# Two layers of cross attention and mixture of experts on one core: a group's whole chain placed ahead of the other group's expert blocks

## The reference, cut to what matters

```
x = x + xattn0(layernorm(x), ctx)      # 16 heads of 8, rope, masked softmax
x = x + ffn0(layernorm(x))             # 32 routed experts of 64 and 8 empty ones, top 6
x = x + xattn1(layernorm(x), ctx)      # 1 head of 128, padding mask; V is the context itself
x = x + ffn1(layernorm(x))             # below

def ffn1(x):
    xn  = rms_norm(x, scale)
    ids = argmin(dist2(xn, centroids))            # one of 8 experts for each token
    for e in range(8):
        a, g = split(xn @ up_w[e])                # 128 -> 2 x 256
        y = (a * silu(g)) @ down_w[e]             # 256 -> 128
        out = where(ids == e, y, out)
    return out + x
```

## Time and profile before

| | us |
|---|---|
| runs | 311.01, 307.35, 305.27 (median 307.35) |
| the profiled execution | 305.88 |
| its span | 304.1 |
| TensorE busy | 258.1 (85%) |
| VectorE busy | 182.0 (60%) |
| ScalarE busy | 123.9 (41%) |
| GpSimd busy | 86.4 (28%) |
| mean TensorE clock | 0.907 of full speed |

### The profile page before, as it was taken

How to read it: one execution, slowest core, us unless ns; L and a number is a source line. 1 busy time by engine, 2 the same in 40 slices (tenths; PEclk the granted TensorE clock), 3 DMA queues, 4 the chain that set the end, 5 groups by cost and what they waited for, 6 DMA issues and landing times.

```text
span 304.1 us, 4365 instructions
## 1 busy us (share of the span) xinstructions
PE 258.1 (85%) x1420; PEld 159.7 (53%) x1420; DVE 182.0 (60%) x486; ACT 123.9 (41%) x244; POOL 86.4 (28%) x100
## 2 busy tenths in 40 slices
PE   3554989989999999998999999999876795867990
PEld 2331335435544544556666666677532565756880
DVE  5922679556656873539868659557862345623540
ACT  1111001454555558684664343562703516323640
POOL 6339022312211110101431301001433005576363
PEclk9955557999999999999999999999998797889996
DMA  6698860822731400045766543532143500162000
GB/s 191 235 168 197 147 107 21 216 45 77 161 49 66 138 0 10 2 129 181 218 204 198 166 159 110 167 91 87 36 154 109 143 0 2 41 193 70 11 22 5
DMA packets 21590, 32.90 MB, mean 108 GB/s; under 512 B 3456, under 2 KB 13896, under 8 KB 20448
## 3 DMA queue, kind: packets, MB, share of 16 engines
q1 hardware_dynamic: 19184, 25.76, 32.3%
q10 hardware_dynamic: 1296, 5.24, 5.9%
q0 software_dynamic: 1088, 1.61, 1.6%
HBM read 28.70 MB, written 7.73 MB: 120 GB/s over the span
## 4 chain that ended last, share of the span: by engine, by line
PE 65%; DVE 12%; DMA 8%; ACT 5%; issue 4%; POOL 2%; SPq 2%; DVEq 0%; POOLq 0%; ACTq 0%
PE psum L1178 59%; DMA big<-qk_scratch 4%; DMA qk_scratch<-parts 3%; DVE negmax L1110 2%; PE psum L1449 2%; ACT early L746 1%; DMA late<-ctx_t 1%; PE psum L1221 1%; DVE stats L831 1%; DVE xres L1017 1%; DVE xs L1046 1%; POOL rms L535 1%; PE psum L1266 1%; POOL out L610 1%; SPq L428 1%
## 5 line engine op out<-in xcount | busy, mean ns | idle before, releaser
L1178 PE MATMUL psum<-xs,ws 128*128 128x512 f32 x192 | 58.7, 441 | 0.0
L1110 DVE TENSOR_REDUCE negmax<-psum 128x4 f32<-128x1024 f32 x32 | 39.1, 1222 | 21.7 <-PE psum L1178 21.5
L1178 PE MATMUL psum<-maskb,id 128*128 128x512 bf16 x128 | 43.3, 424 | 2.0 <-DVE negmax L1110 2.0
L746 ACT ACTIVATE early<-psum 128x1024 f32<-128x1024 f32 x32 | 32.7, 1025 | 28.8 <-PE psum L1178 28.7
L1178 PEld LDWEIGHTS psum<-xs,ws 128*128 128x128 f32 x192 | 35.3, 188 | 15.7 <-issue 9.8
L1178 PEld LDWEIGHTS psum<-big 32*128 32x128 f32 (+1 forms) x256 | 21.2, 205 | 37.9 <-issue 30.4
L1178 PE MATMUL psum<-big 32*128 32x256 f32 (+1 forms) x256 | 35.4, 357 | 6.1 <-DMA big<-qk_scratch 6.1
L1178 PE MATMUL psum<-hid,wdown 128*128 128x512 f32 x64 | 32.4, 593 | 0.0
L774 ACT ACTIVATE psum<-psum 128x512 f32<-128x512 f32 x32 | 18.7, 583 | 28.0 <-PE psum L1178 27.7
L1134 DVE TENSOR_TENSOR hid<-early,psum 128x512 f32<-128x512 f32 x32 | 22.0, 687 | 2.7 <-ACT psum L774 1.7
L1128 DVE TENSOR_TENSOR early<-late,psum 128x512 f32<-128x512 f32 x22 | 15.1, 684 | 13.9 <-PE psum L1178 11.7
(11 more groups left out here) (216 smaller groups left out, 420.9 us busy)
## 6 DMA issues: line engine op xcount, KB each, us to landing
late<-route SPq DMA_DIRECT2D x44, 128.0 KB, 3.0
late<-experts ACTq DMA_DIRECT2D x8, 512.0 KB, 4.6
big<-qk_scratch SPq DMA_DIRECT2D x24, 128.0 KB
row_blocks<-fill SPq DMA_DIRECT2D x22, 132.0 KB, 2.9
early<-route SPq DMA_DIRECT2D x20, 128.0 KB, 3.0
qk_scratch<-parts SPq DMA_DIRECT2D x16, 128.0 KB, 2.9
big<-qk_scratch SPq DMA_DIRECT2D x16, 64.0 KB
wdown<-experts ACTq DMA_DIRECT2D x1, 1024.0 KB, 4.9
```

The costliest lines, as they stand in the source:

```text
L746: nc.scalar.activation(probs[:, t % 4, :, :, :], psum[:, b_bank(t):b_bank(t) + 2, :].rearrange("p r (k q) -> p r k q", k=QT), ACT.Exp).the ...
L1110: nc.vector.tensor_reduce(negmax[:, b % 2, :, :].rearrange("p t (r j) -> p r t j", r=2)[:, :, :, j], psum[:, bank:bank + 2, :].rearrange(" ...
L1178: return nc.tensor.matmul(o, w, r, start=start, stop=stop, skip_group_check=True)
```

## The change

The chain of the second group, from pv1 to rank and rows, moves on all four engines ahead of block 0 of the first group, and xb0 of the first group moves behind it. xb1 and xb2 move to other turns. `weights_of(1)` moves from the front of block 8 to right behind rank. Behind yT stand 16 products in place of 12, behind xT3 and q1 two each (new), behind oproj1 12 in place of 8. In each turn of TensorE the down product now comes ahead of the transposes. In the second group ScalarE's cast waits for the first four, eight or eleven ups (by its number) of the first group, where it waited for all eleven; the copy of the token numbers on VectorE moves from turn 2 to turn 1.

```diff
@@ -110,10 +110,10 @@
 
 ENGINES = ("pe", "act", "dve", "pool")
 BESIDE_BLOCKS = ({"yT": (0, 0, 0, 0), "norm2": (0, 0, 0, 0), "xT3": (0, 0, 0, 0), "q1": (0, 0, 0, 0), "s1": (0, 0, 0, 0),
-                  "s1_": (0, 0, 0, 0), "xb0": (0, 0, 0, 0), "pT": (0, 0, 0, 0), "pT_": (0, 0, 0, 0), "pv1": (1, 1, 1, 1),
-                  "oproj1": (4, 4, 3, 3), "norm3": (5, 4, 3, 4), "skip": (5, 5, 5, 5), "xb1": (5, 5, 5, 5), "xT4": (7, 7, 7, 7),
-                  "dist": (8, 8, 8, 8), "rank": (11, 11, 9, 8), "rows": (11, 11, 11, 9), "xb2": (17, 17, 17, 17)},
-                 {"xb0": (0, 0, 0, 0), "xb1": (1, 1, 1, 1), "xb2": (5, 5, 5, 5)})
+                  "s1_": (0, 0, 0, 0), "pT": (0, 0, 0, 0), "pT_": (0, 0, 0, 0), "pv1": (0, 0, 0, 0), "oproj1": (0, 0, 0, 0),
+                  "norm3": (0, 0, 0, 0), "skip": (0, 0, 0, 0), "xT4": (0, 0, 0, 0), "dist": (0, 0, 0, 0), "rank": (0, 0, 0, 0),
+                  "rows": (0, 0, 0, 0), "xb0": (0, 0, 0, 0), "xb1": (4, 4, 4, 4), "xb2": (17, 17, 17, 17)},
+                 {"xb0": (0, 0, 0, 0), "xb1": (7, 7, 7, 7), "xb2": (13, 13, 13, 13)})
 
 
 def slot_tasks(s):
@@ -733,7 +733,7 @@
                     n_cols = P * (min(4 * c + 4, BLOCKS) - 4 * c)
                     act.wait_ge(misc_full, misc_index(task) + 1)
                     if b == 1:
-                        act.wait_ge(blk_u, BLOCKS)
+                        act.wait_ge(blk_u, min(4 * c + 4, BLOCKS))
                     nc.scalar.copy(xbT[c][:, 0, 0:n_cols], m[:, 0:n_cols]).then_inc(blk_xhi, 1)
 
             for s in range(SLOTS):
@@ -1153,7 +1153,7 @@
                         misc_task(name, b)
                     for name, b in block_tasks(g, "dve", 3 * i + 2):
                         misc_task(name, b)
-                    if i == 2:
+                    if i == 1:
                         dve.wait_ge(blocks_in[g][2], 16)
                         nc.vector.tensor_copy(token_i[:, g, :], row_blk[g][:, :, 2 * D]).then_inc(token_ready, 1)
                     if i >= 2:
@@ -1477,21 +1477,23 @@
                         misc_task(*task)
                         if task == ("yT", 1):
                             weight_at[0] = weights_of(0)
+                            keep_busy(16)
+                        if task in (("xT3", 1), ("q1", 1)):
+                            keep_busy(2)
+                        if task == ("oproj1", 1):
                             keep_busy(12)
-                    if (g, i) == (0, 8):
-                        weight_at[1] = weights_of(1)
+                        if task == ("rank", 1):
+                            weight_at[1] = weights_of(1)
                     if i < BLOCKS:
                         block_up(g, i, weight_at[g][i])
                     for task in block_tasks(g, "pe", 3 * i + 1):
                         misc_task(*task)
-                        if task == ("oproj1", 1):
-                            keep_busy(8)
+                    if i >= 2:
+                        block_down(BLOCKS * g + i - 2, weight_at[g][i - 2])
+                    for task in block_tasks(g, "pe", 3 * i + 2):
+                        misc_task(*task)
                     if 1 <= i <= BLOCKS:
                         hidden_turned(BLOCKS * g + i - 1)
-                    for task in block_tasks(g, "pe", 3 * i + 2):
-                        misc_task(*task)
-                    if i >= 2:
-                        block_down(BLOCKS * g + i - 2, weight_at[g][i - 2])
 
 
 def rope_tables():
```

## The result

The changed kernel takes 314.47 us (median of 4 runs, 313.83 to 315.94), the kernel before in the same comparison 308.01. The ratio is 1.029, with a 95% interval from 1.024 to 1.034: slower by nearly 3%. The same kernel measured again on another chip gave 1.024 (1.019 to 1.029). In some executions a kernel runs slower at a lower clock; the ratios, and the medians in the table of the experiments, are of the other executions alone. I had forecast 310.0, a ratio of 1.009. The direction was right and the time lies inside the range, near its upper end, but the loss is 6.5 us by the two medians and 7 to 9 us by the two ratios, where I forecast 2.7: two and a half to three times as much.

A forecast was written before the change was run, and what follows sets the result against it. Bound by a latency chain whose holes the blocks fill, then by TensorE's own work. First up 20.3 us later, first group's blocks 15.0 instead of 32.9, passage +0.25: +2.7 on 307.35 gives 310.0 us, range 304.5 to 315.5.

The forecast's parts named there:

- the order is worth nothing: Down product ahead of the transposes: no effect inside a beat, about 0.45 us at the turn between the groups.
- the low clock over the blocks: First group's blocks start at the low clock for 3.3 us, a loss of 1.6 us.
- the stop for the loads: Between rank and xb0 TensorE idles while eleven register loads pass: 2.1 us, ends 0.97 and 2.6.
- the later xb1 and xb2: Second group's xb1 and xb2 come one beat or more ahead of their block in both versions; no cost counted.
- my own sign: In the timeline: first up near 262; the forecast is wrong if it comes ahead of 259 or behind 265.
- The chain and the holes: Second group's chain, without blocks in its holes, gets 5 us shorter; the first up comes 20.3 us later.
- the rows of the second group were no use: Second group's rows are written by 262, six us earlier, but wanted only at 280: no gain.
- rival (b): Clock falls early and stays low over chain and first blocks: +6.9 us, so 317; chance 0.17.
- The clock in the chain: High for s1 and s1_ (pv1 starts 4.1 us earlier), pv1 at 2.46 us, dist low at 1.87 us.
- rival of a held clock (a): Added products keep 2.4 GHz to the end of the chain: -3.3 us, so 306.7; chance 0.17.

The follow-up runs named there:

- turn_first: Changed kernel with the transposes ahead of the down product again in each turn; 312.77 us, ratio 1.019 against the kernel before.
- clock_held: Changed kernel with more products that nobody reads in the chain's idle places on TensorE; 309.76 us, ratio 1.016 against the kernel before.
- order_alone: Kernel before with only the changed kernel's table of places (BESIDE_BLOCKS); 309.59 us, ratio 1.021; run again as order_alone_2: 311.63 us, ratio 1.015.
- side_edits_mended: Changed kernel with transposes ahead of the down product, loads behind xb0, weight_i's numbers 16 words apart; 308.9 us, ratio 1.006 against the kernel before.

## Why the prediction was right in its direction and too small

The direction came from a mechanism that the traces bear out; four terms of the sum failed. The one with a wrong argument is "the order is worth nothing": the order of the turn cost about 1.8 us in the blocks and the passage, where I had 0.45 (turn_first takes it back). The others are mis-sized: the low clock over the blocks (1.6 us taken, 3.4 measured), the stop for the loads (2.1 taken, 3.1 measured), and the later xb1 and xb2, put at nothing (0.4 measured in the second group). By my own sign the first profile was wrong too: its first up came at 265.4, behind 265.

- **The chain and the holes: right.** s1 began 9.1 us behind yT as forecast, its four records took 1.13 at the high clock, and the rows of the second group were no use (I had them loaded from 262 on; it was 265.94). The first up came 20.3 us later by the forecast and 22.5 by the trace (21.0 in the second profile).
- **The loads: mis-sized.** "nothing covers them here, so I take 2.1, ends 0.97 and 2.6": from the end of weight_i to xb0 it was 3.1 us in both profiles, above my upper end. The sequencer's load had its own row, 2.89 us, in the trace of before, and I read only TensorE's idle; a part of the load had lain under products still running. +1.0.
- **The order of a turn: wrong.** "the order is worth nothing (bounds: none either way ...)". A TensorE that is 98% busy doesn't show that its records could not be longer or later: 0.08 us on each full beat, +0.5 in the second group at the same clock, about as much in the first, and +0.8 in the passage, where I had 0.45 against a row that was itself 0.2 slow from the clock. Together near 2 us; the time says 1.7.
- **The clock over the blocks: low by half.** I gave it 1.6 us in the first group and nothing in the second. The first four beats took 7.6 us where the same beats at full clock take 5.2 (clock_held), so near 2.3, and the second group lost 1.1. That is rival (b) in part, in a place that I hadn't named.
- **The clock in the chain: nearly a draw.** pv1 took 3.4 us, not the 2.46 taken (in the second profile 2.0); dist took 1.03, the time of the high clock, and not 1.87. These cancel. But pv1 began 15.4 us behind yT in both profiles, and I had 14.7 (239.05): the high clock over s1 gained 3.4 us up to pv1 and not 4.1. The end of weight_i came 1.1 us later than forecast in the first profile and 0.4 earlier in the second.
- **xb1 and xb2: overlooked.** I let them stand for nothing. At the same clock and the same order of a turn the second group takes 13.8 us with them later (turn_first, and order_alone, where only the table changed) and 13.4 in the kernel before, where they lie in the first beats, while the row of engines fills: 0.4.

Over the forecast this makes, from yT: +2.2 to the first up, +1.5 in the first group, +0.4 in the passage, +2.0 in the second group, +0.1 behind it. These 6.2 us, with 1.1 from ahead of yT and the 2.7 forecast, are the ten of the spans. The rival of a held clock (a) was refuted for this kernel, and clock_held shows what it would have been worth.

What stays open is how much the move costs by itself: the runs leave it between nothing (side_edits_mended, with added products and quick loads) and 3% (order_alone). Executions of one program differ by as much as the terms here, and their mean clock doesn't tell why: order_alone_2 took 309.3 us at 0.967, but 310.6 and 313.1 us at 0.901 and 0.902.

## What to carry to other kernels

A chain of latency with holes and a stretch that fills TensorE should lie beside each other or, if one goes first, nothing should separate them: no wait that the next work doesn't need, and no register load in front of it. That products queued one behind the other leave no gap doesn't say that their order is free: compare the beat in a trace of each order. Price a register load from the sequencer's own row and not from the idle time around it. And where a pipeline of blocks runs twice, try joining the two loops: of the three edits tried alone on the kernel before it was the only one that made it faster (3.3 us of passage and second group in the trace, 1% of the time).

## What the runs showed of the hardware that I had not expected

- A load of eleven numbers into TensorE's registers takes 1.5 us or 2.9 us by where they lie: at words 0 to 10 of the tile 1.5, at words 11 to 21 2.7 to 3.0, at words 16 to 26 1.3 to 1.5. It was so in every profile, whatever stood around the load. Which border the words at 11 cross was not tried. The Trainium skill, page "Runtime: NRT & Kernel Launch", section "Instruction fetch mechanics", has about 200 ns for each register, for the loads that the runtime puts in; here it was 120 to 140 or 240 to 270 by the place, so one figure doesn't cover it.
- Two orders of the same products differ by 6% of the beat (1.36 and 1.44 us) though TensorE shows no idle time in either. What differs in the rows is when the weight loads start: 0.25 us late behind the up, at once behind the transposes.
- The load can pass under queued products: in clock_held the 20 products behind rank leave only 1.24 us of "issue" idle ahead of xb0, with a load of 2.89 us that begins before they end. It saves no time there: xb0 still starts 3.1 us behind the end of weight_i (255.85), as in the changed kernel. The rows, TensorE's timeline and the sequencer's loads of clock_held:

```profile
253.24 4.48 PE L1178 MATMUL psum<-all 128*128 128x512 bf16 x20
...
258.95 0.63 PE L1289 MATMUL psum<-id,early 128*128 128x128 f32 x4 [1.24 <-issue]
```

```profile
L1423 PEldq TENSOR_LOAD <-weight_i x2: 1518/2202/2887, 222.8 to 255.9; - x2
```
